# Layer 1's bias rows in three vector operations on all partitions, and new orders of work on three engines, in a fused GroupNorm, Hadamard and pointwise-MLP kernel

## The chip, the cores and the metric

One core of a Trainium2 chip runs the kernel. The metric is the time of one execution on the device in microseconds, lower is better. In the profile PE is TensorE's matmuls, PEld its weight loads, DVE VectorE, ACT ScalarE, POOL GpSimd and SP SyncE, which issues the DMAs.

## What is computed

The input x has 16 images of 192 channels and 56 x 56 points in fp32. The function is a pair of residual stages:

```
x  = x + hadamard(gn(x))           # per point: 192 channels times a Hadamard matrix
x1 = gn(x)                         # GroupNorm, 32 groups of 6 channels, no affine part
h  = gelu(layernorm(x1 @ W1.T + b1) * g1 + beta1)     # over the 192 channels of a point
h  = gelu(layernorm(h  @ W2.T + b2) * g2 + beta2)
out = x + (h @ W3.T + b3)
```

## The kernel before

**Tiling.** Two images make a pair (8 pairs). A pair's 192 channels lie as three blocks of columns: the first 128 channels of either image, and the last 64 of both, one image on the lower 64 partitions and one on the upper. A pair's 3136 points are cut into 7 units of 448, 56 units in all. Every fp32 operand of a matmul is split into an fp16 part and an fp16 remainder ("hi", "lo"); ACT makes the hi parts, DVE and POOL the lo parts.

**Stages of a unit.** Load; `stats_x` (DVE, GroupNorm 1's statistics, one instruction for each block); `scaled_hi` (ACT) and `scaled_lo` (DVE) make the scaled input `xs`; `h_ab` and `h_c` (PE) are the Hadamard matmuls; `residual` (DVE) adds them into X; `stats_x1` (DVE) is GroupNorm 2's statistics; `split_x1` (ACT) and `x1_split_lo` (DVE) make `x1`; then two layers, each in halves h = 0, 1 of 224 points: `group` (PE), `squares` (ACT), `rstd` (POOL), `normalise` (DVE), `transposes` (PE), `gelu` and `gelu_hi` (ACT), `gelu_lo` (POOL). `l3_ab` and `l3_c` (PE) are layer 3, `final_ab` and `final_c` (DVE) add them to X, and SP stores.

**The order.** Each engine runs a prologue (the first pair's GroupNorm 1, all its Hadamard units, the weights' preparation) and then `step(g)` for g = 0 to 57. A step's list of calls is written out by hand for each engine, and semaphores tie the lists together. Step g holds layer 1 of unit g, layer 2 of unit g - 1, layer 3 of unit g - 2 and the Hadamard stage of unit g + 8 (steps 6 to 47). Steps 2 and 4 hold a second Hadamard unit, named by `FIRST_H` in slot k = 1. The 21 statistics instructions 42 to 62 are dealt to steps 1 to 3 by `FIRST_STATS`.

**Shapes on PE.** The bias matmul (L402), L409, L320 and L356 work in tiles of 64 rows; L337 and L373 in tiles of 64 columns; L415, L315, L332, L351, L368 and the fp32 transposes (L427, L433) use the full height and width (112 rows for the transposes). PSUM has two banks `tm` for the layers, two `tp` for the transposes, and two `hl`, called "a" and "b", that the Hadamard stage, layer 3 and GroupNorm's small products share; `free` waits until the last reader of a bank is done.

**GroupNorm at a pair's border.** Once in seven steps each norm has its own work. GroupNorm 1 of pair q (steps 4, 11, 18, 25, 32, 39): `gn_stats` (DVE), `gn_means` (PE), `gn_var` (DVE), `groupnorm_rstd` (POOL), `gn_shift` (DVE), and in the next step `h_shift` (PE) and `gn_h_bias` (DVE). GroupNorm 2 (steps 6, 13, 20, 27, 34, 41, 48): the same chain, then `w1_shift` (PE) multiplies the shift by W1, and `gn_w1_bias` (DVE) makes layer 1's two bias rows (hi and lo) from it, on partitions 0, 1, 64 and 65. The next pair's first `group` (L402) waits for `s_bias` and for `s_x1_lo`. `ones` is one on those four partitions only, and zero elsewhere. The parameter column `row1` is 1 on partitions 1 and 65, so a row comes out as value minus hi on odd and as value on even ones, with the sign turned once more at the end.

Of the kernel before, what the change touches and what calls it, by code (L numbers as in the profile page):

```python
# [83 lines left out]
def build(nc, x, weights, biases, params, consts, out):  # L84
    ctx = ExitStack()
    with ctx:
# [575 lines left out]
        def _(dve):  # L662
# [141 lines left out]
            def gn_shift(q, n):  # L804

                if q is None:
                    return
# [3 lines left out]
                mu = gmu[:, 0, :]
                if n == 1:
                    do(nc.vector.tensor_tensor(gmu_b3[:, :], mu, b3, ALU.add))
                    mu = gmu_b3[:, :]
# [228 lines left out]
```

## Time and profile before

| what | value |
|---|---|
| time, median of 3 runs | 1047.11 us (1045.45 to 1048.05) |
| the profiled execution | 1043.52 us |
| its span, first to last instruction | 1041.7 us |
| PE busy | 932.8 us, 90% |
| ACT busy | 890.1 us, 85% |
| DVE busy | 868.4 us, 83% |
| POOL busy | 612.5 us, 59% |
| mean granted TensorE clock | 0.977 of full |
| DMA | 80.66 MB, mean 77 GB/s |

The span is what the trace covers, and the profiled execution took 1.8 us more than it. An engine's busy time is a mean over a prologue, 58 steps of several kinds and a tail, so the rows of single steps say more than the table.

### The profile page before, as it was taken

How to read it: one execution, taken by the hardware profiler on the slowest of the kernel's cores; microseconds unless marked ns; L12 is line 12 of the kernel's file. 1: busy time of each engine (PE TensorE's matmuls, PEld its weight loads, DVE VectorE, ACT ScalarE, POOL GpSimd, SP SyncE). 2: the span in 40 equal slices, each digit the busy share in tenths (PEclk: the TensorE clock that was granted, in tenths of full speed). 3: DMA queues.
4: the chain of work that ended last, by engine and by line, in shares of the span. 5: the costliest groups of instructions: out<-in, count | busy, mean ns of one | idle time of the engine just before them, and what ended most of it. 6: DMA issues, size and time to landing. Idle time of an engine off the chain costs nothing.

```text
span 1041.7 us, 25024 instructions
## 1 busy us (share of the span) xinstructions
PE 932.8 (90%) x9384; PEld 638.9 (61%) x9384; DVE 868.4 (83%) x1553; ACT 890.1 (85%) x2821; POOL 612.5 (59%) x477
## 2 busy tenths in 40 slices
PE   0637898999998999999998999999999999999995
PEld 0216565666666666666765666666676666677662
DVE  6798999998999899999899989999889877854542
ACT  0727887899988998899988998889998999899992
POOL 0533654566665667556665667566665666666662
PEclk9967999999999999999999999999999999999997
DMA  9524021132222222222322232222101111011111
GB/s 288 158 78 109 28 81 55 54 107 77 85 81 81 81 81 86 77 85 78 107 71 74 85 94 81 81 81 81 54 31 52 34 50 54 28 54 55 54 46 62
DMA packets 49080, 80.66 MB, mean 77 GB/s; under 512 B 5568, under 2 KB 48704, under 8 KB 48832
## 3 DMA queue, kind: packets, MB, share of 16 engines
q1 hardware_dynamic: 48960, 79.06, 24.8%
q8 instruction: 75, 1.23, 0.5%
q14 instruction: 45, 0.37, 0.1%
HBM read 40.51 MB, written 38.54 MB: 76 GB/s over the span
## 4 chain that ended last, share of the span: by engine, by line
PE 68%; DVE 22%; POOL 3%; ACT 2%; issue 2%; SPq 1%; DMA 1%; POOLq 0%; ACTq 0%; DVEq 0%
PE tm L415 18%; PE tp L427 9%; PE tm L409 8%; PE tm L402 5%; PE hl L351 5%; PE hl L315 4%; DVE z L871 3%; PE hl L373 3%; PE tp L433 3%; PE hl L356 3%; PE hl L368 3%; DVE X L745 3%; DVE bn L720 3%; DVE x_lo L861 2%; PE hl L320 2%; DVE xs_lo L736 2%
## 5 line engine op out<-in xcount | busy, mean ns | idle before, releaser
L626 POOL TENSOR_TENSOR ge_lo<-ge,ge_hi 128x672 f16<-128x672 f32 x224 | 334.5, 1494 | 131.4 <-ACT ge_hi L532 131.4
L617 POOL TENSOR_TENSOR rs<-ssq,neg_half 112x4 f32<-112x4 f32 x224 | 246.6, 1101 | 228.0 <-ACT z L503 228.0
L503 ACT ACTIVATE z<-tm 112x194 f32<-112x194 f32 x896 | 284.3, 340 | 29.0 <-PE tm L415 29.0
L871 DVE TENSOR_TENSOR z<-tm,rs 112x768 f32<-112x768 f32 x224 | 212.6, 949 | 55.7 <-POOL rs L617 54.2
L516 ACT ACTIVATE ge<-tp,par 128x448 f32<-128x448 f32 x224 | 163.6, 731 | 53.6 <-PE tp L427 45.6
L503 ACT ACTIVATION_READ_ACCUMULATOR z<-tm 112x1 f32 x896 | 194.9, 217 | 0.0
L532 ACT ACTIVATE ge_hi<-ge 128x672 f16<-128x672 f32 x224 | 174.4, 778 | 2.2
L427 PE MATMUL tp<-cst,z 112*128 112x112 f32 x896 | 134.9, 273 | 14.8 <-DVE z L871 13.0
L745 DVE SCALAR_TENSOR_TENSOR X<-hl,h_bias,X 128x448 f32<-128x448 f32 x161 | 105.0, 678 | 50.4 <-PE hl L320 42.3
L427 PEld LDWEIGHTS tp<-cst,z 112*128 112x128 f32 x896 | 89.5, 142 | 87.8 <-issue 59.6
L494 ACT ACTIVATE x_hi<-X,gscale 128x448 f16<-128x448 f32 x168 | 106.8, 671 | 21.2 <-DVE gscale L819 21.2
L519 ACT ACTIVATE ge<-tp,par 128x224 f32<-128x224 f32 x224 | 121.0, 540 | 0.0
L415 PE MATMUL tm<-w_hi,x_hi 128*112 128x192 f16 x448 | 116.2, 259 | 0.0
L415 PE MATMUL tm<-w_hi,ge_hi 128*112 128x192 f16 x448 | 115.1, 257 | 0.0
L736 DVE SCALAR_TENSOR_TENSOR xs_lo<-X,gscale,xs_hi 128x448 f16<-128x448 f32 x150 | 114.4, 769 | 0.8 <-ACT xs_hi L483 0.7
L415 PE MATMUL tm<-w_lo,x_hi 128*112 128x192 f16 x448 | 111.2, 248 | 0.0
L415 PE MATMUL tm<-w_hi,x_lo 128*112 128x192 f16 x448 | 111.1, 248 | 0.0
L861 DVE SCALAR_TENSOR_TENSOR x_lo<-X,gscale,x_hi 128x448 f16<-128x448 f32 x168 | 109.9, 683 | 1.2 <-ACT x_hi L494 0.9
L415 PE MATMUL tm<-w_lo,ge_hi 128*112 128x192 f16 x448 | 110.2, 246 | 0.0
L415 PE MATMUL tm<-w_hi,ge_lo 128*112 128x192 f16 x448 | 110.2, 246 | 0.0
L483 ACT ACTIVATE xs_hi<-X,gscale 128x448 f16<-128x448 f32 x150 | 99.9, 676 | 5.5 <-DVE gscale L819 5.5
L720 DVE BATCH_NORM_STATS2 bn<-X 128x6 f32<-128x448 f32 x168 | 100.0, 617 | 5.3 <-DMA X<-x 5.1
(138 smaller groups left out, 2181.5 us busy)
## 6 DMA issues: line engine op xcount, KB each, us to landing
X<-x SPq DMA_DIRECT2D x56, 448.0 KB, 3.7
out<-X SPq DMA_DIRECT2D x56, 448.0 KB, 2.7
X<-x SPq DMA_DIRECT2D x112, 112.0 KB, 3.7
out<-X SPq DMA_DIRECT2D x112, 112.0 KB, 2.8
X<-weights SPq DMA_DIRECT2D x1, 1024.0 KB, 12.2
cst<-consts SPq DMA_DIRECT2D x1, 704.0 KB, 9.7
X<-biases SPq DMA_DIRECT2D x1, 192.0 KB, 2.5
par<-params SPq DMA_DIRECT2D x1, 6.5 KB, 1.6
```

Of the source, the lines that this page charges most:

```text
L415: last = nc.tensor.matmul(dst[:, i, k * TW:k * TW + C], act[:, buf, i, cols], w[:, 3 * i, :], start=False, stop=(r == 2), skip_group_check ...
L427: last = nc.tensor.transpose(tp[:, 0, i * HALF + k * TT:i * HALF + (k + 1) * TT], z[n][:, 2 * h + k, at:at + 128], ident[0:TT, 0:TT])
L503: last = nc.scalar.activation(z[n][:, 2 * h + k, i * TW:(i + 1) * TW], tm[h][:, i, k * TW:(k + 1) * TW], ACT.Square, scale=float(C) ** -0. ...
L516: nc.scalar.activation(ge[n][:, 0:2, cols], tp[:, 0, 0:2 * HALF].rearrange("p (b t) -> p b t", b=2), ACT.Gelu, bias=par[:, 4 * n + 2:4 * n ...
L532: nc.scalar.activation(ge_hi[n][:, g % 2, :, cols], ge[n][:, :, cols], ACT.Copy).then_inc(s_ge_hi[n], 1)
L617: nc.gpsimd.tensor_tensor(rs[n][:, 2 * h:2 * h + 2, :], ssq[n][:, 2 * h:2 * h + 2, :], neg_half[0:TT, 0:4].rearrange("p (i k) -> p i k", i=2),
L626: nc.gpsimd.tensor_tensor(ge_lo[n][:, g % 2, :, cols], ge[n][:, :, cols], ge_hi[n][:, g % 2, :, cols], ALU.subtract).then_inc(s_ge_lo[n], 1)
L720: ins = nc.vector.bn_stats(bn[0][:, (a // U) % 2, b, a % U, :], xcols(a, b))
L736: ins = nc.vector.scalar_tensor_tensor(out=xs_lo[:, a % 2, b, :], in0=xcols(a, b), scalar=scale1(a // U, b), in1=xs_hi[:, a % 2, b, :], op ...
L745: nc.vector.scalar_tensor_tensor(out=xcols(a, b), in0=tp[:, 0, 0:UT] if b == 2 and a < U else hl[:, b % 2, 0:UT], scalar=h_bias[:, (a // U ...
L861: ins = nc.vector.scalar_tensor_tensor(out=x1_lo[:, g % 2, b, :], in0=xcols(g, b), scalar=gscale2[:, b:b + 1], in1=x1_hi[:, g % 2, b, :], ...
L871: nc.vector.tensor_tensor(z[n][:, 2 * h:2 * h + 2, 0:2 * C].rearrange("p k (i o) -> p i k o", i=2), tm[h][:, :, 0:2 * TW].rearrange("p i ( ...
```

## The change

Five edits. (1) `gn_w1_bias` works on all 128 partitions in three operations: subtract, cast to fp16, and one `scalar_tensor_tensor` that writes both copies of the rows; the parameter column is -1 where it was 1. `layer_biases` in the prologue is shortened the same way. (2) The shift has the other sign, so `gn_shift` needs no multiplication by -1; for GroupNorm 2 it adds `b3` in the same instruction, three instead of one and six. (3) The prologue has 7 instead of 10 statistics instructions ahead of step 0 and 14 instead of 11 in it, fewer of them ahead of `gn_var`, and makes the bias rows before the first `x1_split_lo`. (4) POOL's first `groupnorm_rstd(0, 1)` comes after the last weight remainder, no longer before it. (5) The step lists of PE, ACT, POOL and DVE are reordered.

```diff
-FIRST_STATS = {0: (42, 42), 1: (42, 52), 2: (52, 56), 3: (56, 63)}
+FIRST_STATS = {0: (42, 42), 1: (42, 54), 2: (54, 54), 3: (54, 63)}
 # PE step
     group(g, 0, 0)
+    transposes(g - 2, 1, 1)
     h_ab(h_unit(g, 0))
-    transposes(g - 2, 1, 1)
     group(g, 0, 1)
...
     transposes(g, 0, 1)
+    group(g - 1, 1, 1)
     w1_shift(gn2_pair(g))
-    group(g - 1, 1, 1)
     h_shift(h_shift_pair(g))
     l3_c(g - 2)
+    transposes(g - 1, 1, 0)
     h_ab(h_unit(g, 1))
-    transposes(g - 1, 1, 0)
     h_c(h_unit(g, 1))
 # ACT step: scaled_hi of slot 0 moves: block 0 between the first two squares,
 # block 2 behind gelu(g, 0, 0), ahead of split_x1(g + 1, 0); slot 1 is spread out
 # POOL step
     gelu_lo(g - 2, 1, 1)
+    rstd(g, 0, 1)
     groupnorm_rstd(gn2_pair(g), 1)
-    rstd(g, 0, 1)
 # DVE step, after the change
+    gn_stats(gn2_pair(g), 1)
+    first_stats(g)
+    gn_stats(gn1_pair(g), 0)
+    scaled_lo(xs_unit(g, 0), 0)
+    residual(h_unit(g, 0), 0)
+    residual(h_unit(g, 0), 1)
+    normalise(g, 0, 0)
+    stats_x1(h_unit(g, 0), 0)
+    stats_part(g, 0)
+    gn_var(gn2_pair(g), 1)
+    residual(h_unit(g, 0), 2)
+    gn_var(gn1_pair(g), 0)
+    scaled_lo(xs_unit(g, 0), 1)
+    gn_shift(gn2_pair(g), 1)
+    normalise(g, 0, 1)
+    scaled_lo(xs_unit(g, 0), 2)
+    x1_split_lo(g + 1, 0)
+    x1_split_lo(g + 1, 1)
+    final_ab(g - 2)
+    stats_x1(h_unit(g, 0), 1)
+    normalise(g - 1, 1, 0)
+    gn_shift(gn1_pair(g), 0)
+    scaled_lo(xs_unit(g, 1), 0)
+    gn_w1_bias(gn2_pair(g))
+    x1_split_lo(g + 1, 2)
+    gn_h_bias(h_shift_pair(g))
+    stats_part(g, 1)
+    final_c(g - 2)
+    normalise(g - 1, 1, 1)
+    stats_x1(h_unit(g, 0), 2)
+    residual(h_unit(g, 1), 0)
+    stats_part(g, 2)
+    scaled_lo(xs_unit(g, 1), 1)
+    residual(h_unit(g, 1), 1)
+    residual(h_unit(g, 1), 2)
+    stats_x1(h_unit(g, 1), 0)
+    scaled_lo(xs_unit(g, 1), 2)
+    stats_x1(h_unit(g, 1), 1)
+    stats_x1(h_unit(g, 1), 2)
 # gn_w1_bias, after the change
+    nc.vector.tensor_tensor(b_row[:, :], b32[:, :], gp[:, 0:C], ALU.subtract).then_inc(s_gread, 1)
+    dve.wait_ge(s_gread, reads)
+    do(nc.vector.tensor_copy(b_hi[:, :], b_row[:, :]))
+    nc.vector.scalar_tensor_tensor(out=bias_rows[0][:, :, 0:C],
+                                   in0=b_hi[:, :].unsqueeze(1).to_broadcast([128, 2, C]), scalar=low_row,
+                                   in1=b_row[:, :].unsqueeze(1).to_broadcast([128, 2, C]),
+                                   op0=ALU.mult, op1=ALU.add).then_inc(s_bias, 1)
 # DVE prologue
-            stats_x(range(21, 27))
+            stats_x(range(21, 24))
             gn_var(0, 1)
-            stats_x(range(27, 28))
+            stats_x(range(24, 26))
             gn_shift(0, 1)
-            stats_x(range(28, 31))
+            stats_x(range(26, 28))
+            gn_w1_bias(0)
             for b in range(3):
                 x1_split_lo(0, b)
-            gn_w1_bias(0)
```

## Rows read from the trace of the kernel before

**Rows 1.** Busy us by stretch: length, PE, PEld, DVE, ACT, POOL; then clock, DMA.
```profile
92.62:189.56 96.94, 85.25 (x833) 57.51 (x832) 89.06 (x150) 79.75 (x254) 50.36 (x40) 0.97 0.14 44
225.94:241.72 15.78, 15.78 (x166) 10.84 (x165) 13.99 (x22) 15.48 (x51) 10.28 (x9) 1.00 0.28 89
510.07:528.14 18.07, 16.87 (x172) 11.70 (x171) 16.70 (x34) 15.57 (x51) 13.11 (x11) 1.00 0.25 77
544.76:564.13 19.37, 17.64 (x181) 12.05 (x180) 18.20 (x52) 16.11 (x51) 10.37 (x10) 1.00 0.24 73
564.13:581.13 17.00, 15.95 (x164) 10.83 (x164) 16.58 (x24) 15.27 (x51) 9.89 (x8) 1.00 0.27 82
926.44:940.94 14.50, 13.58 (x150) 10.09 (x149) 7.32 (x10) 13.91 (x48) 9.73 (x9) 1.00 0.15 49
```
**Rows 2.** Timeline of PE, step 29: start us, us, engine, line, operation, tiles.
```profile
582.88 0.25 PE L415 MATMUL tm<-w_hi,x_lo 128*112 128x192 f16 x1
582.96 0.35 PE L315 MATMUL hl<-xs_hi,h 128*128 128x448 f16 x1
...
584.01 0.35 PE L320 MATMUL hl<-xs_lo,h 64*128 64x448 f16 x2
...
584.73 0.35 PE L433 MATMUL tp<-cst,z 112*128 112x112 f32 x2
585.02 0.37 PE L402 MATMUL tm<-bias,ones 64*112 64x388 f16 x2
```
**Rows 3.** Timeline of PE, steps 1 and 48, other neighbours of the same blocks.
```profile
96.87 0.35 PE L320 MATMUL hl<-xs_lo,h 64*128 64x448 f16 x2
97.06 0.33 PE L402 MATMUL tm<-bias,ones 64*112 64x388 f16 x2
...
896.79 0.55 PE L427 MATMUL tp<-cst,z 112*128 112x112 f32 x4
897.18 0.35 PE L433 MATMUL tp<-cst,z 112*128 112x112 f32 x2
```
**Rows 4.** Timelines of PE, DVE and POOL at pair 4's border, steps 27 and 28.
```profile
559.15 0.83 PE L296 MATMUL hl<-w,gshift 128*2 128x192 f32 x8 [1.49 <-DVE X L883]
...
560.32 0.70 DVE L841 TENSOR_TENSOR b_row<-hl,b 2x192 f32<-2x192 f32 x2
563.39 0.68 DVE L861 SCALAR_TENSOR_TENSOR x_lo<-X,gscale,x_hi 128x448 f16<-128x448 f32 x1
563.99 1.89 DVE L736 SCALAR_TENSOR_TENSOR xs_lo<-X,gscale,xs_hi 128x448 f16<-128x448 f32 x1
567.52 0.94 DVE L871 TENSOR_TENSOR z<-tm,rs 112x768 f32<-112x768 f32 x1
...
563.86 1.53 POOL L626 TENSOR_TENSOR ge_lo<-ge,ge_hi 128x672 f16<-128x672 f32 x1
```
**Rows 5.** Timelines of DVE and PE in step 25, GroupNorm 1 of pair 5.
```profile
522.37 2.42 DVE L817 SCALAR_TENSOR_TENSOR gshift<-gmu,gscale 128x2 f32<-128x2 f32 x3
...
526.03 0.36 PE L368 MATMUL hl<-ge_hi,w_hi 128*128 128x448 f16 x1 [1.20 <-DVE X L883]
```
**Rows 6.** Timeline of DVE, operations of the new rows' kinds, in the prologue.
```profile
5.16 0.26 DVE L691 CAST bias<-X 128x192 f16<-128x192 f32 x1
5.46 0.42 DVE L692 SCALAR_TENSOR_TENSOR X<-bias,par,X 128x192 f32<-128x192 f16 x1
```
**Rows 7.** Timeline of DVE, from the first pair's GroupNorm 2 into step 0.
```profile
66.56 0.15 DVE L797 COPY gmu<-hl 128x8 f32<-128x8 f32 x1
...
68.44 1.10 DVE L813 TENSOR_TENSOR gmu_b<-gmu,par 128x4 f32<-128x4 f32 x1 [0.60 <-POOL gscale L609]
...
76.68 5.89 DVE L720 BATCH_NORM_STATS2 bn<-X 128x6 f32<-128x448 f32 x11
```
**Rows 8.** Timelines of DVE and PE at the end of step 2, slot k = 1.
```profile
126.78 3.45 DVE L736 SCALAR_TENSOR_TENSOR xs_lo<-X,gscale,xs_hi 128x448 f16<-128x448 f32 x3
...
130.89 0.36 PE L332 MATMUL hl<-xs_hi,h 128*128 128x448 f16 x1 [1.80 <-DVE X L745]
```

More of the change, by code:

```diff
@@ L729, in first_stats @@
                 if g == 0:
-                    stats_x(range(31, 42))
+                    stats_x(range(28, 42))
             def scaled_lo(a, b):
@@ L807, in gn_shift @@
                     return
-                do = chain(q, n, 2)
                 dve.wait_ge(s_grs, gn_use(q, n) + 1)
                 scale = (gscale1[:, q % 2, :], gscale2[:, :])[n]
[L811 to L814, printed above, removed]
-                for rows, cols in ((slice(0, 128), slice(0, 2)), (lower[0], slice(2, 3)), (lower[1], slice(3, 4))):
-                    for i in range(n + 1):
-                        nc.vector.scalar_tensor_tensor(out=gshift[n][rows, cols, i], in0=mu[rows, cols], scalar=-1.0,
-                                                       in1=scale[rows, cols], op0=ALU.mult, op1=ALU.mult)
+                for rows, cols, w in ((slice(0, 128), slice(0, 2), 2), (lower[0], slice(2, 3), 1), (lower[1], slice(3, 4), 1)):
+                    if n == 0:
+                        nc.vector.tensor_tensor(gshift[0][rows, cols, 0], gmu[rows, 0, cols], scale[rows, cols], ALU.mult)
+                    else:
+                        shape = [rows.stop - rows.start, w, 2]
+                        nc.vector.scalar_tensor_tensor(out=gshift[1][rows, cols, :],
+                                                       in0=gmu[rows, 0, cols].unsqueeze(2).to_broadcast(shape),
+                                                       scalar=b3[rows, cols.start:cols.start + 1],
+                                                       in1=scale[rows, cols].unsqueeze(2).to_broadcast(shape),
+                                                       op0=ALU.add, op1=ALU.mult)
                 nc.vector.tensor_copy(scale[lower[1], 2:3], scale[lower[1], 3:4]).then_inc(s_gn[n], 1)
@@ L837, in gn_w1_bias @@
                 dve.wait_ge(s_gred, reads)
-                do = chain(q, 1, 3)
-                two = (slice(0, 2), slice(64, 66))
-                for rows in two:
-                    last = nc.vector.tensor_tensor(b_row[rows, :], gp[rows, 0:C], b32[rows, :], ALU.add)
-                last.then_inc(s_gread, 1)
-                dve.wait_ge(s_gread, reads)
-                for rows in two:
-                    last = nc.vector.tensor_copy(bias_rows[0][rows, 0, 0:C], b_row[rows, :])
-                do(last)
-                for rows in two:
-                    last = nc.vector.scalar_tensor_tensor(out=b_row[rows, :], in0=bias_rows[0][rows, 0, 0:C],
-                                                          scalar=row1[rows, :], in1=b_row[rows, :],
-                                                          op0=ALU.mult, op1=ALU.subtract)
-                do(last)
-                for rows in two:
-                    for k in range(2):
-                        last = nc.vector.tensor_scalar(bias_rows[0][rows, k, 0:C], b_row[rows, :], -1.0, None, ALU.mult)
-                last.then_inc(s_bias, 1)
+                do = chain(q, 1, 2)
+                nc.vector.tensor_tensor(b_row[:, :], b32[:, :], gp[:, 0:C], ALU.subtract).then_inc(s_gread, 1)
+                dve.wait_ge(s_gread, reads)
+                do(nc.vector.tensor_copy(b_hi[:, :], b_row[:, :]))
+                nc.vector.scalar_tensor_tensor(out=bias_rows[0][:, :, 0:C],
+                                               in0=b_hi[:, :].unsqueeze(1).to_broadcast([128, 2, C]), scalar=low_row,
+                                               in1=b_row[:, :].unsqueeze(1).to_broadcast([128, 2, C]),
+                                               op0=ALU.mult, op1=ALU.add).then_inc(s_bias, 1)
             def x1_split_lo(g, b):
@@ L906, in step @@
                 gn_shift(gn2_pair(g), 1)
-                stats_part(g, 0)
                 normalise(g, 0, 1)
+                scaled_lo(xs_unit(g, 0), 2)
                 x1_split_lo(g + 1, 0)
                 x1_split_lo(g + 1, 1)
-                gn_shift(gn1_pair(g), 0)
                 final_ab(g - 2)
```

52 lines of the change are left out of this document (20 added, 32 removed).

## The prediction

> **What bounds the kernel now.** I read the timeline of PE first and took the start of each unit's first bias matmul (L402) as the start of its step. That splits the span into a prologue of 76.8 us, steps 0 to 55 (938.5 us, nine tenths) and a tail. Then I read busy time by step. The stretches of [rows 1] are steps 1 to 5 together, then steps 8, 25, 27, 28 and 50. In a plain step, such as step 8, PE is busy for all of the 15.78 us, ACT for 15.48 and DVE for 13.99 [rows 1]. So PE sets the pace of a plain step, and only fewer or closer matmuls shorten it; ACT stands right behind. Of the 42 steps 6 to 47, those with Hadamard work, 20 are of this kind and length. The steps at a pair's border are longer, and there PE does wait: 19.37 us with 17.64 busy in step 27, 17.00 with 15.95 in step 28, and 18.07 with 16.87 in step 25 [rows 1]. Steps 1 to 5 take 96.94 us with PE busy for 85.25 and DVE for 89.06, so neither is full alone [rows 1]. From step 49 on there is no Hadamard work and a step takes 14.50 us with 13.58 of PE [rows 1]; there a chain of latencies rules, and its lists are the same before and after, since all calls that move are empty in those steps. I give these steps and the tail nothing.
>
> **Term 1, the order on PE in each Hadamard step.** The transposes of unit g - 2 move from behind h_ab to ahead of it. No matmul is removed, so only the gaps between neighbours can change. From the last L415 of the first group to L402 of the second it now takes 585.02 - 582.88 = 2.14 us [rows 2]. From the last L320 over four transposes to L433 it is 0.72, of which four transposes behind a group take 0.39; 0.33 are left, although the distance from L320 to L402, where those two are neighbours, is 0.19 [rows 2, 3]. L433 to L402 is 0.29 for two transposes, which by the 0.39 for four take about 0.2 [rows 2, 3]. In every case the longer gap stands where the matmul shape goes from 64-row tiles to the full array or back, and the full-to-full change L415 to L315 costs its plain 0.08 [rows 2]. In the new order the sum is 0.08 (group to transposes) + 0.39 + 0.22 to 0.29 (L433 to h_ab, no row shows it; 0.22 if it has no gap, like other full neighbours) + 1.05 (L315 to the last L320, unchanged) + 0.19 = 1.93 to 2.00. That is 0.14 to 0.21 us less; I take 0.18, as two of three gaps are read directly. For 42 steps: 7.6 us. The lower bound is 0, if the gap only moves. The page "TensorEngine Tiling (Array Packing)" of the Trainium skill, section Key Properties, says that changing the tiling mode drains the engine; by counting changes, 16 in a step become 14, it would give about the same.
>
> Do the others keep up at 15.60 us? ACT's 15.48 leaves 0.12. But it includes overlaps of neighbouring instructions, and its list is the same in sum. DVE first waits for h_ab, which now ends 0.7 us later in the step; it does one scaled_lo of 0.6 before it, so it loses nothing of its 1.8 us of slack. final_ab comes 0.6 us later, behind scaled_lo block 2; l3_c has 1.3 us between l3_ab's product being added and its own start, so it isn't delayed.
>
> **Term 2, the border of GroupNorm 2 (steps 6/7 to 41/42, six times).** Three waits. w1_shift waits 1.49 us for final_ab to free bank "b", with group(g-1, 1, 1) queued behind it [rows 4]. In the new list that group (1.83 us from its L402 on) goes first and covers the wait. gn_w1_bias took from 560.32 to 563.39 = 3.07 us of DVE [rows 4], with x1_split_lo block 2 behind it, for which the next group waits. New: the subtraction as one of L841's two, 0.35; the cast 0.26 [rows 4, 6]; the wide one has 384 elements, 0.42 for 192 [rows 6] to 0.84 for twice that, and I take 0.61, on the slope from 192 elements to the 448 of L861's 0.68 [rows 4]; with two waits of 0.04, 1.3 us. gn_shift saves some 0.4 more by four fewer small instructions. So DVE has 2.2 us less to do, and w1_shift starts 14.4 us into the step, as before. I walked the new lists with these durations: normalise(g, 0, 1) moves up by 1.1 us, since POOL's rstd now precedes the GroupNorm's; w1_shift ends 15.2 us after the step's start, bias rows are there at 16.6, x1_lo block 2 at 17.2, while PE itself is done at 17.25. The wait is gone to within 0.1. In step 28 PE waited 1.05 us, 17.00 less 15.95 [rows 1], at h_ab, because DVE was late: normalise at 567.52, behind a scaled_lo that took 1.89 instead of 0.68 [rows 4]. DVE's 2.2 us, and normalise(g-1, 1, 1) ahead of the statistics, put that at 1.9 us into the step, where PE asks for it at 1.8. A border then costs two plain steps plus PE's own small products: 36.37 becomes 33.5 before term 1, so 2.7 us saved, and 2.3 at 41/42, where no statistics run: 5 x 2.7 + 2.3 = 15.8. Bounds: 0 if each wait only moves, 3.1 a border if all goes.
>
> **Term 3, the border of GroupNorm 1 (steps 11, 18, 25, 32).** gn_shift took 2.42 us for three tiny instructions, and final_ab, queued behind it, held up l3_c by 1.20 us [rows 5]. Now final_ab, a statistic and a normalise stand ahead of it. What waits next is x1_split_lo block 2, 1.4 us before it is needed. 4 x 1.2 = 4.8 us; step 39 shows no such wait.
>
> **Term 4, step 48.** w1_shift waits as in step 27, 1.5 us [rows 4], and the step after it shows no wait that the change touches: 1.5.
>
> **Term 5, the prologue.** gn_var, now at 66.56, comes three statistics earlier; at 5.89 / 11 = 0.535 us each [rows 7] that is 1.6 us at most, of which I take 1.1, since GroupNorm's means on PE must be done first. gn_shift's first operation took 1.10 us for 0.16 of work, under POOL's last weight remainder [rows 7]; with edit (4) that is over before: 0.9. The merged shift gives 0.4 and the rows 1.8. Against it stand three statistics more in step 0, 1.6 us. 1.1 + 0.9 + 0.4 + 1.8 - 1.6 = 2.6 us. Edit (4) also lets SP, which waits for the last weight remainder, issue the third pair's loads some 9 us earlier; the statistics already find their data, so nothing more comes of it. layer_biases lies ahead of the first unit's landing: 0.
>
> **Term 6, steps 1 to 5.** In steps 2 and 4 three scaled_lo (3.45 us with a stall) stand between h_ab of the second unit and its residual, and h_c waits 1.80 us for it [rows 8]. Two of the three are now behind the residual. PE waited for 96.94 - 85.25 = 11.7 us in the five steps, DVE for 96.94 - 89.06 = 7.9 [rows 1]. The longer list is DVE's: 89.06, of which 2.8 are stalls of the two trios (3.45 each, where three at 0.68 take 2.04). Of its 7.9 us idle some half waits for step 1's first h_ab and stays. So 89.1 + 3.9 = 93.0 if the stalls stay, 90.2 if not; I take 92.5, a gain of 4.4 us, with bounds of 0 and 8.
>
> **The sum.** 7.6 + 15.8 + 4.8 + 1.5 + 2.6 + 4.4 = 36.7 us. The span of 1041.7 becomes 1005.0 and the profiled execution's 1043.52 becomes 1006.8. The median of the runs shown is 3.6 above that execution, so 1010.4; I say 1011.
>
> **Rivals.**
> *The waits move (A).* POOL's gelu_lo and DVE meet: the scaled_lo at 563.99 took 1.2 us more beside the gelu_lo from 563.86 [rows 4], while most others ran undisturbed. If the wide bias instruction, x1_split_lo behind it or the moved gn_shift meets it at each border, 1.2 us comes back at seven GroupNorm 2 borders (8.4), and steps 1 to 5 give nothing (4.4): 1011 + 12.8 = 1024. For it speaks that bias rows are now ready 1.9 us after w1_shift is issued, on the path; against it, that the walk puts POOL's gelu_lo elsewhere by 1 us. The Trainium skill, "GPSIMD Engine Reference", Key points, says GpSimd shares its SBUF interfaces with VectorE instructions that have two SBUF inputs, which the wide one has on 128 partitions. It speaks against edit (1), and the row above agrees.
> *The gaps stay (B).* If the gap of 0.1 belongs to the transposes and not to the change of shape, term 1 is 0: 1018.6. ACT as the new bound gives nearly the same: at 15.7 us a step, 0.1 of the 0.18 is lost in 42, and the time is 1015.
> *Slower (C).* The new PE list puts h_ab behind transposes that wait for normalise(g-2, 1, 1). So a loop closes in every step: that normalise, transposes 0.66, h_ab 1.24, then DVE from residual to the next such normalise, 13.99 less two statistics and one scaled_lo = 12.35, and latencies 0.3: 14.55 us. It is 1.05 under the 15.60 of PE. One stall of 1.2 us in the loop lengthens a step to 15.75 and eats term 1 alone; from two a step (16.95, 1.17 above before) the loss is 42 x 1.17 = 49 against the other terms' 29: 1067. It decides from 29 / 42 = 0.7 us above 15.78. Against it: in plain steps the trace shows scaled_lo at 0.68 to 0.78, one near-miss a step.
> *The change does nothing (D).* It would need A at full size and term 1 at 0 and 15 us more; I see no single mechanism.
>
> **How the numbers follow.** Forecast (all six terms near their size) 0.63, own range 1004 to 1018. A 0.17, B 0.11, D 0.03, C 0.06. The range that leaves out no more than 2 in 10 runs from 1001 (term 6 at its bound of 8, borders at 3.1, term 1 at 0.21: 5 to 8 us more) to 1026 (A). What a measurement of this kernel can tell from no change is about 0.3%, 3 us. Faster by more 0.91, within 0.03, slower 0.06.
>
> **What the profile after would show.** Step 8's kind at 15.57 to 15.64 us with PE full (term 1); L433 to L315 at 0.22. L296 without a wait, and borders of GroupNorm 2 at some 33.0 us for two steps. Step 25's kind at 16.7. First L402 near 72.5 and step 1 near 90.0. Wrong would be: plain steps above 15.8 with PE waiting at L427 for z (C); L402 of steps 7, 14, ... waiting for bias or x_lo by over 0.5 us (A); plain steps still 15.78 (B).

## The result, and the profile after

The changed kernel takes 1005.14 us (median of 4 runs, 1004.59 to 1005.64) against 1047.58 us before (median of 4 runs, 1045.45 to 1048.12). The ratio is 0.9598, with a 95% interval of 0.9582 to 0.9615: 4.0% faster. The profiled execution took 1005.64 us with a span of 1003.7; before they were 1043.52 and 1041.7. The spans differ by 38.0 us. The line numbers of the loop moved by a few: L402 is L404, L415 L417, L427 L429, L433 L435, L315 L317, L320 L322, L296 L298, L272 L274; L736 stays, L861 is L854, L871 L864, L883 L876.

Busy time by stretch, in the columns of [rows 1]: steps 1 to 5, then steps 8, 25, 27, 28 and 50, each from its first L404 to the next step's.

```profile
91.68:187.33 95.65, 86.51 (x832) 60.17 (x832) 87.76 (x153) 79.27 (x254) 51.86 (x40) 0.94 0.15 45
220.22:235.71 15.49, 15.49 (x164) 10.90 (x163) 14.05 (x22) 15.34 (x51) 9.75 (x9) 1.00 0.30 90
490.89:507.28 16.39, 16.39 (x173) 11.80 (x172) 15.88 (x36) 15.45 (x51) 11.16 (x10) 1.00 0.28 85
523.61:540.86 17.25, 17.25 (x181) 12.07 (x180) 16.87 (x39) 15.56 (x51) 10.26 (x9) 1.00 0.27 81
540.86:556.50 15.64, 15.64 (x165) 10.93 (x165) 15.05 (x23) 15.45 (x51) 9.78 (x9) 1.00 0.29 89
888.45:902.94 14.49, 13.58 (x150) 10.08 (x149) 7.30 (x10) 13.89 (x48) 9.71 (x9) 1.00 0.15 49
```

In all four steps of the loop PE is now busy from end to end. The plain step fell from 15.78 to 15.49 us, step 25 from 18.07 to 16.39, step 27 from 19.37 to 17.25 and step 28 from 17.00 to 15.64; step 50 did not move. ACT, at 15.34 of 15.49, is right behind PE. Steps 1 to 5 gave only 1.29 us, and their granted clock is 0.94 where it was 0.97.

The timeline of PE in step 30, which answers to [rows 2]:

```profile
573.74 0.25 PE L417 MATMUL tm<-w_hi,x_lo 128*112 128x192 f16 x1
573.82 0.55 PE L429 MATMUL tp<-cst,z 112*128 112x112 f32 x4
574.21 0.35 PE L435 MATMUL tp<-cst,z 112*128 112x112 f32 x2
574.40 0.35 PE L317 MATMUL hl<-xs_hi,h 128*128 128x448 f16 x1
...
575.45 0.35 PE L322 MATMUL hl<-xs_lo,h 64*128 64x448 f16 x2
575.64 0.33 PE L404 MATMUL tm<-bias,ones 64*112 64x388 f16 x2
```

From the last L417 to L404 it is now 575.64 - 573.74 = 1.90 us, where [rows 2] had 2.14. The transposes hand over to h_ab in 0.19 and h_ab's 64-row tiles to the 64-row bias matmul in 0.19.

The border of pair 4, which answers to [rows 4], on DVE and, last, on PE:

```profile
538.90 0.35 DVE L842 TENSOR_TENSOR b_row<-b,hl 128x192 f32<-128x192 f32 x1
539.29 0.26 DVE L844 CAST b_hi<-b_row 128x192 f16<-128x192 f32 x1
539.58 0.62 DVE L845 SCALAR_TENSOR_TENSOR bias<-b_hi,par,b_row 128x384 f16<-128x384 f16 x1
540.12 0.68 DVE L854 SCALAR_TENSOR_TENSOR x_lo<-X,gscale,x_hi 128x448 f16<-128x448 f32 x1
...
540.86 0.37 PE L404 MATMUL tm<-bias,ones 64*112 64x388 f16 x2
```

The bias rows take 540.12 - 538.90 = 1.22 us, where they took 3.07 [rows 4], and no line of PE in steps 27 and 28 shows idle time ahead of it.

PE in the prologue and step 0, with its idle time and what ended it in brackets:

```profile
73.29 0.57 PE L404 MATMUL tm<-bias,ones 64*112 64x388 f16 x2 [3.25 <-DVE x_lo L854]
82.15 1.87 PE L274 MATMUL hl<-gst,cst 128*128 128x4 f32 x8 [2.53 <-DVE gst L789]
85.78 0.98 PE L429 MATMUL tp<-cst,z 112*128 112x112 f32 x4 [0.53 <-DVE z L864]
```

The first step starts 3.5 us sooner (73.29, was 76.80), but then PE waits 2.53 us for the statistics (1.11 before), and its next eight small matmuls take 1.87 us, where the same eight took 1.05 before: the granted clock over them is 0.50, the lower of its two levels, and was 1.00. Step 1 starts at 91.68, only 0.94 sooner than the 92.62 of [rows 1].

### The profile page after: what moved, and what is told of

It is laid out like the page before. It is cut to its first block, busy times and chain, and to the rows that moved or that the text cites. A ratio compares the mean times of both kernels' runs of the same rounds, so it can differ in the third digit from the quotient of the medians.

```text
span 1003.7 us, 24928 instructions
## 1 busy us (share of the span) xinstructions
PE 921.3 (92%) x9384; PEld 645.5 (64%) x9384; DVE 839.9 (84%) x1462; ACT 883.2 (88%) x2821; POOL 595.9 (59%) x477
## 4 chain that ended last, share of the span: by engine, by line
PE 80%; DVE 9%; ACT 4%; POOL 3%; issue 1%; SPq 1%; DMA 1%; POOLq 0%; ACTq 0%
PE tm L417 22%; PE tp L429 10%; PE tm L411 10%; PE hl L353 6%; PE tm L404 5%; PE hl L317 4%; PE hl L375 4%; PE hl L358 4%; PE tp L435 4%; PE hl L370 3%; PE hl L322 2%; PE hl L339 2%; PE hl L334 2%; DVE bn L720 2%; PE hl L274 2%; POOL ge_lo L628 2%
## 5 line engine op out<-in xcount | busy, mean ns | idle before, releaser
L619 POOL TENSOR_TENSOR rs<-ssq,neg_half 112x4 f32<-112x4 f32 x224 | 234.5, 1047 | 251.7 <-ACT z L505 251.5
L628 POOL TENSOR_TENSOR ge_lo<-ge,ge_hi 128x672 f16<-128x672 f32 x224 | 328.6, 1467 | 90.6 <-ACT ge_hi L534 90.5
L864 DVE TENSOR_TENSOR z<-tm,rs 112x768 f32<-112x768 f32 x224 | 212.6, 949 | 57.7 <-POOL rs L619 56.2
L505 ACT ACTIVATION_READ_ACCUMULATOR z<-tm 112x1 f32 x896 | 203.8, 227 | 0.0
L534 ACT ACTIVATE ge_hi<-ge 128x672 f16<-128x672 f32 x224 | 176.7, 789 | 2.2
L429 PE MATMUL tp<-cst,z 112*128 112x112 f32 x896 | 133.3, 271 | 13.5 <-DVE z L864 12.3
L429 PEld LDWEIGHTS tp<-cst,z 112*128 112x128 f32 x896 | 91.1, 143 | 69.4 <-issue 39.4
L736 DVE SCALAR_TENSOR_TENSOR xs_lo<-X,gscale,xs_hi 128x448 f16<-128x448 f32 x150 | 107.0, 716 | 27.1 <-ACT xs_hi L485 27.0
L521 ACT ACTIVATE ge<-tp,par 128x224 f32<-128x224 f32 x224 | 123.1, 550 | 0.0
L417 PE MATMUL tm<-w_hi,x_hi 128*112 128x192 f16 x448 | 116.7, 261 | 0.0
L417 PE MATMUL tm<-w_hi,ge_hi 128*112 128x192 f16 x448 | 115.6, 258 | 0.0
L417 PE MATMUL tm<-w_lo,x_hi 128*112 128x192 f16 x448 | 111.7, 249 | 0.0
L417 PE MATMUL tm<-w_hi,x_lo 128*112 128x192 f16 x448 | 111.7, 249 | 0.0
L854 DVE SCALAR_TENSOR_TENSOR x_lo<-X,gscale,x_hi 128x448 f16<-128x448 f32 x168 | 109.9, 682 | 1.8 <-ACT x_hi L496 1.6
L417 PE MATMUL tm<-w_hi,ge_lo 128*112 128x192 f16 x448 | 110.7, 247 | 0.0
L417 PE MATMUL tm<-w_lo,ge_hi 128*112 128x192 f16 x448 | 110.7, 247 | 0.0
```

The source lines that it names most:

```text
L417: last = nc.tensor.matmul(dst[:, i, k * TW:k * TW + C], act[:, buf, i, cols], w[:, 3 * i, :], start=False, stop=(r == 2), skip_group_check ...
L429: last = nc.tensor.transpose(tp[:, 0, i * HALF + k * TT:i * HALF + (k + 1) * TT], z[n][:, 2 * h + k, at:at + 128], ident[0:TT, 0:TT])
L505: last = nc.scalar.activation(z[n][:, 2 * h + k, i * TW:(i + 1) * TW], tm[h][:, i, k * TW:(k + 1) * TW], ACT.Square, scale=float(C) ** -0. ...
L521: nc.scalar.activation(ge[n][:, 2, cols], tp[:, 1, 0:HALF], ACT.Gelu, bias=par[:, 4 * n + 3:4 * n + 4], scale=par[:, 4 * n + 1:4 * n + 2]) ...
L534: nc.scalar.activation(ge_hi[n][:, g % 2, :, cols], ge[n][:, :, cols], ACT.Copy).then_inc(s_ge_hi[n], 1)
L619: nc.gpsimd.tensor_tensor(rs[n][:, 2 * h:2 * h + 2, :], ssq[n][:, 2 * h:2 * h + 2, :], neg_half[0:TT, 0:4].rearrange("p (i k) -> p i k", i=2),
```

## The experiments

The diffs say from which of the two kernels each one starts. The lists that differ between the two are those of four engines, POOL's by one pair of lines. The table gives the lengths of five kinds of step in the profiled execution, in us, the start of step 6, and the median.

| kernel | 8 | 25 | 27 | 28 | 48 | step 6 starts | median |
|---|---|---|---|---|---|---|---|
| before | 15.78 | 18.07 | 19.37 | 17.00 | 17.19 | 189.56 | 1047.6 |
| after | 15.49 | 16.39 | 17.25 | 15.64 | 15.67 | 187.33 | 1005.1 |
| e1, h_ab first again | 15.78 | 16.67 | 17.54 | 15.78 | 15.64 | 191.59 | 1018.9 |
| e2, before + swap | 15.73 | 19.93 | 19.20 | 19.41 | 17.17 | 195.91 | 1082.3 |
| e3, narrow bias rows | 15.50 | 16.38 | 21.69 | 16.86 | 20.23 | 188.52 | 1053.2 |
| e4, w1_shift early | 15.49 | 16.39 | 18.67 | 15.50 | 17.12 | 187.25 | 1014.3 |
| e5, gn_shift 1 early | 15.50 | 16.38 | 17.24 | 15.65 | 15.67 | 185.06 | 1004.4 |
| e6, 64-row tiles first | 15.74 | 16.63 | 17.49 | 15.89 | 15.67 | 186.99 | 1014.0 |
| e7, old prologue | 15.50 | 16.39 | 17.25 | 15.64 | 15.67 | 183.58 | 1004.5 |
| e8, transposes before l3 | 15.79 | 16.73 | 19.49 | 15.61 | 20.18 | 188.29 | 1035.9 |
| e9, new forms, old lists | 15.78 | 18.06 | 18.83 | 15.78 | 16.97 | 189.05 | 1031.7 |
| e10, e5 and e7 together | 15.50 | 16.39 | 17.25 | 15.64 | 15.66 | 189.96 | 1006.9 |
| e11, e2 + early normalise | 15.74 | 21.18 | 19.09 | 18.88 | 17.18 | 202.47 | 1081.1 |
| e12, changed kernel again | 15.50 | 16.39 | 17.25 | 15.64 | 15.66 | 187.09 | 1004.0 |

### What does the swap on PE give? (e1, e6)

e1 puts h_ab ahead of the transposes again in the changed kernel; e6 keeps the swap and runs h_ab's 64-row tiles before its full ones, so that its neighbours on both sides change shape again.

```diff
 # e1, PE step
     group(g, 0, 0)
-    transposes(g - 2, 1, 1)
     h_ab(h_unit(g, 0))
+    transposes(g - 2, 1, 1)
 # e6, h_ab: the loop over 64-row tiles (start=True) moves ahead of the full ones
```

> The changed kernel with one line of TensorE's step put back: h_ab ahead of the transposes of unit g - 2. Theory (each change of matmul shape costs TensorE a gap of 0.1 us or so, and the new list has two fewer): a plain step goes from 15.50 back to 15.78 us, the whole from 1005 to about 1017. Rival (the plain step became shorter because VectorE's and ScalarE's lists are better): a plain step stays at 15.5 to 15.6, the whole at 1005 to 1009.

> The changed kernel with the inner order of h_ab turned: its matmuls in 64-row tiles first, the full ones last. Same matmuls and neighbours as blocks, two changes of shape more in each Hadamard step. Theory (the gap goes with the change of shape): a plain step of 15.50 becomes 15.70 to 15.78, the whole 1014 to 1017. Rival (the gap belongs to the fp32 transposes or to what stands beside them): no change in the step, 1005.

e1: 1018.9 us, ratio 0.9744 (0.9724 to 0.9764), the plain step back at 15.78. e6: 1014.0 us, 0.9703 (0.9676 to 0.9731), plain step 15.74. PE has no wait in the plain step of either. One order of calls with two more changes of shape costs 0.24 us a step, the whole swap 0.28. In step 30 of e6 both new gaps can be seen:

```profile
579.69 0.35 PE L435 MATMUL tp<-cst,z 112*128 112x112 f32 x2
579.98 0.36 PE L318 MATMUL hl<-xs_hi,h 64*128 64x448 f16 x2
...
581.04 0.35 PE L322 MATMUL hl<-xs_lo,h 128*128 128x448 f16 x1
581.32 0.37 PE L404 MATMUL tm<-bias,ones 64*112 64x388 f16 x2
```

Both handovers took 0.19 in the changed kernel; they are 0.29 and 0.28 here. The transposes stand at the same place in both kernels, so the gap belongs to the change of shape and not to the transposes. That is the rule that the prediction named from the Trainium skill, "TensorEngine Tiling (Array Packing)", section Key Properties (changing the mode drains the engine); the runs agree with it.

### Is the loop of rival C real? (e2, e11)

e2 makes only the swap in the kernel before. e11 moves one line of DVE's list in it as well, the late normalise.

```diff
 # e2 and e11, PE step of before
     group(g, 0, 0)
+    transposes(g - 2, 1, 1)
     h_ab(h_unit(g, 0))
-    transposes(g - 2, 1, 1)
 # e11 alone, DVE step of before
     final_c(g - 2)
+    normalise(g - 1, 1, 1)
...
-    normalise(g - 1, 1, 1)
     stats_part(g, 2)
```

> The kernel before with only that one pair of TensorE's step swapped: the transposes of unit g - 2 ahead of h_ab. If TensorE's gaps are all that counts, a plain step goes from 15.78 to 15.50 and the whole from 1047.6 to about 1036. If VectorE's old list matters, the loop h_ab, residual, everything up to normalise(g - 1, 1, 1), transposes, h_ab closes at some 13.46 + 0.66 + 1.24 + 0.3 = 15.67 us, and the whole is about 1043.

> The kernel before with the swap on TensorE, and one line of VectorE's list moved: normalise(g - 1, 1, 1) stands directly behind final_c(g - 2) and not near the end of the list. The swap alone made the kernel 36 us slower, with TensorE waiting 2.4 us and 1.2 us for z in the step behind a border. Theory: that is the loop of transposes, h_ab, residual and the late normalise; with the normalise early the transposes find z ready, the plain step is 15.50 us, the steps of the borders come back to about those of before less the gap (17.0 and 17.8 us), and the kernel takes 1031 to 1038 us. Rival: the 36 us come from something else that the swap moves (the release of tp, ScalarE's order, the stall beside GpSimd's ge_lo): over 1050 us, with the steps behind the borders still 19 to 21 us.

e2: 1082.3 us, ratio 1.035 (1.0327 to 1.0373), far beyond both numbers expected. The same swap that is worth 13.8 us in the new lists (1018.9 less 1005.1) costs some 36 in the old ones (1082.3 less 1046.1, the median of before beside it). e2 in step 28, PE first and then DVE:

```profile
592.32 0.60 PE L427 MATMUL tp<-cst,z 112*128 112x112 f32 x4 [2.39 <-DVE z L871]
598.26 0.60 PE L427 MATMUL tp<-cst,z 112*128 112x112 f32 x4 [1.24 <-DVE z L871]
...
587.80 1.89 DVE L736 SCALAR_TENSOR_TENSOR xs_lo<-X,gscale,xs_hi 128x448 f16<-128x448 f32 x1
591.33 0.94 DVE L871 TENSOR_TENSOR z<-tm,rs 112x768 f32<-112x768 f32 x1
594.40 1.28 DVE L745 SCALAR_TENSOR_TENSOR X<-hl,h_bias,X 128x448 f32<-128x448 f32 x2 [1.60 <-PE hl L320]
595.59 1.74 DVE L736 SCALAR_TENSOR_TENSOR xs_lo<-X,gscale,xs_hi 128x448 f16<-128x448 f32 x1
597.26 0.94 DVE L871 TENSOR_TENSOR z<-tm,rs 112x768 f32<-112x768 f32 x1
```

PE asks for z one h_ab earlier, and DVE, late from the border, has it at 592.27. Then DVE itself waits 1.60 us for the later h_ab, because the old list puts the residuals at its top, and the stalled scaled_lo and normalise(g, 0, 0) behind them make PE wait 1.24 more. In step 25 the same order delays gn_stats, which stands behind the residuals, and PE waits 1.25 us for it at L272. Both engines wait for each other in turn.

e11: 1081.1 us, ratio 1.0336 (1.0314 to 1.0357). The theory, that the late normalise closes the loop, failed, and the rival's numbers held. Its step 28 and, last, the plain step 30:

```profile
590.46 1.88 DVE L736 SCALAR_TENSOR_TENSOR xs_lo<-X,gscale,xs_hi 128x448 f16<-128x448 f32 x1
593.46 0.95 DVE L871 TENSOR_TENSOR z<-tm,rs 112x768 f32<-112x768 f32 x1
594.46 0.60 PE L427 MATMUL tp<-cst,z 112*128 112x112 f32 x4 [1.86 <-DVE z L871]
600.40 0.60 PE L427 MATMUL tp<-cst,z 112*128 112x112 f32 x4 [1.24 <-DVE z L871]
...
629.08 1.27 DVE L745 SCALAR_TENSOR_TENSOR X<-hl,h_bias,X 128x448 f32<-128x448 f32 x2 [1.59 <-PE hl L320]
631.87 0.60 PE L427 MATMUL tp<-cst,z 112*128 112x112 f32 x4 [0.17 <-DVE z L871]
```

Its place took 0.53 us off the first wait (2.39 to 1.86), one statistics instruction, and nothing off the second. Even the plain step waits 0.17 us for z(g, 0, 0), and takes 15.74. The other two links stay: residuals and scaled_lo between h_ab and normalise(g, 0, 0), and the border's long DVE work. The new lists have the first scaled_lo and gn_stats ahead of the residuals. That these two moves are what makes the swap pay is not shown.

A part of the 36 us is the clock. e2's steps 21 and 28, in the columns of [rows 1], have the same work:

```profile
463.93:485.03 21.10, 18.70 (x163) 12.86 (x163) 16.48 (x24) 15.48 (x51) 9.38 (x8) 0.84 0.22 67
587.94:607.35 19.41, 15.78 (x163) 10.93 (x164) 17.44 (x24) 15.45 (x51) 9.45 (x8) 1.00 0.23 72
```

Each has a wait of 2.4 us at its first transposes; in step 21 the granted clock fell behind it (0.50 from 468 to 474 us) and the step took 1.7 us more, in step 28 it stayed at 1.00.

### What do the wide bias rows give? (e3, e9)

e3 brings the ten narrow operations back into the changed kernel, on partitions 0, 1, 64 and 65. e9 is the opposite: the new forms (edits 1, 2, 4 and the prologue of edit 3) with every step list and `FIRST_STATS` of before.

```diff
 # e3, gn_w1_bias of the changed kernel: for rows in (slice(0, 2), slice(64, 66))
-    nc.vector.tensor_tensor(b_row[:, :], b32[:, :], gp[:, 0:C], ALU.subtract)     # and the two behind it
+    ...     # 2 tensor_tensor, 2 tensor_copy, 2 scalar_tensor_tensor, 4 tensor_scalar
-LINKS = ((2, 2, 0), (3, 2, 1))
+LINKS = ((2, 2, 0), (3, 2, 2))
```

> The changed kernel with gn_w1_bias on partitions 0, 1, 64 and 65 again, in the ten instructions of before (3.07 us against 1.2). Theory (w1_shift ends 15.2 us into the border step and the bias rows and x1_split_lo block 2 behind it are just in time): the next group waits 1.8 us more at each of seven borders, some 12 us in all, 1017. Rival (VectorE has slack there): under 3 us, 1005 to 1008.

> The kernel before with the new forms alone (bias rows in three wide operations, the shift with the other sign, the new prologue of VectorE), every step list of the four engines and the counts of statistics as they were. Theory, by the terms of the prediction without the swap on TensorE: each of the seven GroupNorm 2 borders gives back the 1.8 us between ten narrow operations (3.07 us) and three wide ones (1.30 us), and the 1.2 us stall of the scaled_lo behind them goes or stays with where ge_lo falls, so 13 to 20 us in all; the plain step stays at 15.78 us: 1027 to 1034 us. Rival 1, the forms carry everything but the swap: the whole of the border terms and of the prologue, 26 us and more, 1018 to 1021 us. Rival 2, the new forms only pay with the new lists, since the border waits for something else in the old ones (X of final_ab, 1.49 us): under 7 us, 1039 to 1047 us.

e3: 1053.2 us, ratio 1.0082 (1.006 to 1.0104), slower than before and 48 us above the changed kernel, some 7 us for each of seven borders, where the operations alone differ by 1.8. Its border on DVE, POOL and PE, and the two microseconds behind it in the columns of [rows 1]:

```profile
562.75 2.25 DVE L851 SCALAR_TENSOR_TENSOR b_row<-bias,par,b_row 2x192 f32<-2x192 f16 x2
565.03 2.06 DVE L857 TENSOR_SCALAR bias<-b_row 2x192 f16<-2x192 f32 x4
...
563.34 1.46 POOL L628 TENSOR_TENSOR ge_lo<-ge,ge_hi 128x672 f16<-128x672 f32 x1
565.36 1.46 POOL L628 TENSOR_TENSOR ge_lo<-ge,ge_hi 128x672 f16<-128x672 f32 x1 [0.56 <-ACT ge_hi L534]
...
567.86 0.57 PE L404 MATMUL tm<-bias,ones 64*112 64x388 f16 x2 [4.38 <-DVE x_lo L864]
...
568.00:570.00 2.00, 2.00 (x18) 1.66 (x19) 1.99 (x4) 0.00 (x0) 0.00 (x0) 0.50 0.04 13
```

The rows took 567.12 - 561.46 = 5.66 us and not 3.07. L851's pair and L857's four took 0.83 and 0.89 in the kernel before; here each pair or four met one ge_lo of POOL (over at 564.80 and 566.82) and ended 0.2 to 0.3 us after it, at 565.00 and 567.09. x_lo and PE stand behind them, PE idles 4.38 us, and the clock falls to half. So 1.8 us of work and 2.6 of stall made the border step 4.4 us longer, 21.69 for 17.25. The slow clock made the step behind it 1.2 us longer here and 2.1 to 2.8 at the five other borders of this kind (it took 17.69 to 18.41 us there, with PE busy throughout and a clock of 0.83 to 0.87). The three wide operations are over before the next ge_lo begins, at 541.04 in the changed kernel.

e9: 1031.7 us, ratio 0.9863 (0.9843 to 0.9884), in the range expected (1027 to 1034). Its two border steps:

```profile
538.94:557.77 18.83, 17.50 (x182) 12.04 (x181) 17.81 (x44) 15.79 (x51) 10.06 (x9) 1.00 0.25 74
557.77:573.55 15.78, 15.78 (x165) 10.83 (x165) 13.82 (x22) 15.49 (x51) 10.15 (x9) 1.00 0.28 88
```

They became 34.61 us from 36.37, 1.76 less: 0.54 in step 27, where the wait for x_lo at the end is gone (0.25 us at L402 of step 28 in the kernel before) and the wait at w1_shift is 1.33 us for 1.49, and 1.22 in step 28, where PE's 1.05 us at h_ab is gone with the stall (DVE's scaled_lo took 0.68, no longer 1.89). That the total is near the 1.85 us between the two forms of the rows is thus no proof that it is this difference: most of it is a wait that the stall of scaled_lo had made. The wait at w1_shift and that at layer 3 in step 25 (1.19 us) are still there.

### The moves at the borders (e4, e5)

```diff
 # e4, PE step of the changed kernel
+    w1_shift(gn2_pair(g))
     group(g - 1, 1, 1)
-    w1_shift(gn2_pair(g))
 # e5, DVE step of the changed kernel
+    gn_shift(gn1_pair(g), 0)
     final_ab(g - 2)
...
-    gn_shift(gn1_pair(g), 0)
```

> The changed kernel with w1_shift ahead of group(g - 1, 1, 1), as before. Theory (w1_shift then waits for final_ab to free its bank, with that group behind it): a wait of 1.0 to 1.5 us at seven borders, 7 to 10 us in all, 1012 to 1015. Rival (the earlier bias rows pay for it): 1005 or less.

> The changed kernel with gn_shift of GroupNorm 1 ahead of final_ab again. Theory (its tiny instructions stall beside gelu_lo and hold up final_ab and l3_c): 1.2 us at four or five borders, 5 to 6 us in all, 1010 to 1011. Rival (in the new order GpSimd's work lies elsewhere, so there is no stall): 0 to 1 us, 1005 to 1006.

e4: 1014.3 us, ratio 0.9702 (0.9682 to 0.9722). L298 waits for final_ab's X again, 1.46 us, and the two border steps take 34.17 us, not 32.89. So of the gain at a border, 1.28 is this move and 1.76 the new forms of e9.

e5: 1004.4 us, 0.9607 (0.9586 to 0.9628), and the step of GroupNorm 1 unchanged. In it gn_shift is short although it stands where it stood before:

```profile
500.57 0.39 DVE L813 TENSOR_TENSOR gshift<-gmu,gscale 128x2 f32<-128x2 f32 x3
...
500.72 1.01 POOL L619 TENSOR_TENSOR rs<-ssq,neg_half 112x4 f32<-112x4 f32 x1 [1.85 <-ACT z L505]
501.70 1.47 POOL L628 TENSOR_TENSOR ge_lo<-ge,ge_hi 128x672 f16<-128x672 f32 x1
```

It is over 0.7 us before ge_lo starts, where in [rows 5] it had 2.42 us. The gain of GroupNorm 1's step came with the new lists (e9 does not have it), and in them it does not hang on the place of gn_shift. Whether the move of gn_shift alone would bring it in the old lists is not shown.

### A further order on PE (e8)

```diff
 # e8, PE step of the changed kernel
     group(g - 1, 1, 0)
+    transposes(g, 0, 1)
     l3_ab(g - 2)
-    transposes(g, 0, 1)
     group(g - 1, 1, 1)
```

> The changed kernel with transposes(g, 0, 1) ahead of l3_ab, which takes two more changes of shape out of every step, 0.28 us. But normalise(g, 0, 1) ends about 0.4 us after TensorE would ask for it. If that wait stands in full, a plain step is 15.6 to 15.7 and the whole 1010 to 1014; if the lists shift against each other and ScalarE's 15.2 us of work is the floor, 15.2 to 15.3 and 993 to 997.

1035.9 us, ratio 0.9907 (0.9887 to 0.9926). Neither expectation held. The shapes do fit together, but the transposes lose l3_ab as their cover. The plain step of e8, DVE's normalise(g, 0, 1) and the transposes:

```profile
595.18 0.96 DVE L864 TENSOR_TENSOR z<-tm,rs 112x768 f32<-112x768 f32 x1 [0.24 <-POOL rs L619]
596.19 0.60 PE L429 MATMUL tp<-cst,z 112*128 112x112 f32 x4 [0.36 <-DVE z L864]
```

The transposes start 0.60 us behind the last L417 of the group, 0.52 more than the 0.08 of [rows 2], against the 0.24 that two changes of shape less give back: 15.79 for 15.50. From step 43 to 46 the same wait is 0.74 us and a step takes 16.17; at a border it is 1.12, with 1.12 more for x_lo.

### The prologue (e7, e10, e12)

e7 gives the changed kernel VectorE's old prologue and its counts (10 statistics ahead of step 0, 11 in it); the new forms stay. e10 has the edits of e5 and e7. e12 is the changed kernel once more.

```diff
 # e7 and e10
-                    stats_x(range(28, 42))
+                    stats_x(range(31, 42))
...
-            stats_x(range(21, 24))
+            stats_x(range(21, 27))
             gn_var(0, 1)
-            stats_x(range(24, 26))
+            stats_x(range(27, 28))
             gn_shift(0, 1)
-            stats_x(range(26, 28))
-            gn_w1_bias(0)
+            stats_x(range(28, 31))
             for b in range(3):
                 x1_split_lo(0, b)
+            gn_w1_bias(0)
```

> The changed kernel with the old order in VectorE's prologue: ten statistics ahead of step 0 and eleven in it, bias rows behind x1_split_lo. Edit (4) and the short forms stay. Theory (the new prologue starts step 0 earlier, but VectorE has to do three statistics more in it, and TensorE idles and loses its clock): the first group starts 1.5 to 2 us later, step 1 within 0.5 us of the changed kernel's 91.7, the whole 1004.5 to 1006. Rival (the earlier start reaches the end): 1007.

> The changed kernel with both edits that each gave a microsecond or nothing at the median alone (VectorE's old prologue with its old counts of statistics; gn_shift of GroupNorm 1 ahead of final_ab). Theory: both spare TensorE a fall to the lower clock in steps 0 to 4, and in a place of its own each, so steps 0 and 4 take 15.6 and 23.2 us instead of 18.4 and 25.3, and the rest stays as it is: 3 to 5 us less than the changed kernel, 1000 to 1002 us. Rival: step 4 waits for VectorE whatever stands ahead of it and the old prologue already took that time (its step 4 was 23.7 us), so nothing is added to the old prologue's result: 1003 to 1005 us.

> The changed kernel itself, beside the one with the old prologue on the same chip, to compare these two directly. Nothing is changed. Theory: 1003 to 1006 us, steps 0 and 4 at 18.4 and 25.3 us in the profile if the fall of the clock in the prologue comes back in every execution. Rival: the fall was one execution's, and steps 0 to 5 are shorter by 2 us and more here.

e7: 1004.5 us (1000.6 to 1007.7), ratio 0.9608 (0.9578 to 0.9639). e10: 1006.9 us (1005.0 to 1008.4), 0.9627 (0.9606 to 0.9649). e12: 1004.0 us (1002.7 to 1005.5), 0.9601 (0.9582 to 0.9621). The intervals overlap, so none of the three can be told from another. In e7's profile PE waits less for the statistics, and the eight matmuls behind it still run at the higher clock, unlike the row at 82.15 above:

```profile
80.93 1.05 PE L274 MATMUL hl<-gst,cst 128*128 128x4 f32 x8 [0.54 <-DVE gst L789]
```

Its step 0 takes 15.55 us, not 18.39, and step 1 starts at 89.25. But e10, with the same prologue and a step 0 of 15.54, lost it again: its first step started at 76.37 (73.70 in e7; 1.6 us of the difference stood already behind the first pair's loads), step 1 took 18.03 (17.20 in e12) and step 4 took 26.28 with a clock of 0.79 over 150 to 160 us. The profiled execution of e7 is the fastest of its four and that of e10 the slowest, so their profiles lie further apart than their medians. In e12 steps 0 and 4 came back at 18.39 and 25.25. The changed kernel's fall of the clock in step 0 is thus no accident of one execution, but avoiding it gives nothing at the median.

## Why the prediction was right

The forecast was 1011 us with a range of 1001 to 1026, and 1005.1 was measured, inside the forecast's own range of 1004 to 1018. By its own sum, the profiled execution should have taken 1006.8 us and took 1005.6. So the terms together missed by 1.2 us, and that is in part luck: terms 1 to 3 gave 6.5 us more than foreseen and terms 4 to 6 gave 5.3 less. The forecast's further 3.6 us were added because the median of before lay that far above its profiled execution; after the change the profiled execution lay 0.5 above its median, so this step only took the forecast away from the result. Term by term, from the lengths of the steps in the two traces:

| term | predicted | measured | how measured |
|---|---|---|---|
| 1, order on PE | 7.6 | 11.8 | 0.28 x 42 |
| 2, border of GroupNorm 2 | 15.8 | 17.3 | 5 x (3.49 - 0.56) + 3.16 - 0.56 |
| 3, border of GroupNorm 1 | 4.8 | 5.6 | 4 x (1.68 - 0.28) |
| 4, step 48 | 1.5 | 1.0 | 1.52 less, 0.47 more in step 49 |
| 5, up to step 1 | 2.6 | 0.9 | 92.62 - 91.68 |
| 6, steps 1 to 5 | 4.4 | 1.3 | 96.94 - 95.65 |
| sum | 36.7 | 37.9 | spans: 38.0 |

**Term 1** was right in kind and too small: 0.28 us a step, above its bound of 0.21, and a plain step of 15.49 where 15.57 to 15.64 was expected. L435 to L317 was 0.19, below the 0.22 to 0.29 taken for it, because two transposes take 0.19 and not the 0.2 and more read from [rows 2]. The stretch gave 2.14 - 1.90 = 0.24. Most of the other 0.04 lies behind L404: from L404 to the first L417 it is 0.76 (575.64 to 576.40) where the bias matmul follows a matmul of its own shape, and 0.79 (579.13 to 579.92) where it follows transposes. e6 puts 0.24 of the 0.28 down to the shape. ACT did keep up, with 15.34 us busy. Rival B is refuted by e1 and e6.

**Term 2** is confirmed, also in its parts. The walk had the bias rows ready 16.6 us into the step and x1_lo block 2 at 17.2; in step 27 they were ready at 16.59 and 17.19 (540.20 and 540.80 less 523.61), and the next L404 started at 17.25. 1.76 us of a border come from the new forms (e9), most of it the wait at h_ab that hung on the stall of scaled_lo, and 1.28 from the group ahead of w1_shift (e4). Their sum, 3.04, is about the 2.93 measured beyond term 1.

**Term 3**: the size was near, the reason given for it not borne out. The stall of gn_shift is gone, but it stays gone with gn_shift in its old place (e5). In e5 ge_lo begins only 0.7 us after it, so where ge_lo falls decides, and the other moves had shifted that. Which of their lines did it stays open.

**Terms 5 and 6** failed, 4.8 us too much together. The first step did start 3.5 us sooner, where 4.2 was counted on; of the missing part some 0.5 us is the loads' time: the statistics of the last Hadamard unit ended that much later in the profiled execution of after. Against it the prediction set 1.6 us for three statistics more in step 0. PE's wait there did grow by 1.42, but the prediction left out that the clock can fall behind it, and 2.57 us are spent again in step 0 (18.39 for 15.82). In steps 1 to 5 step 2 gave 1.41 and step 5 1.19, and step 4 took 1.19 back. The wait that term 6 was about did shrink, from 1.80 to 0.86 us in step 2 and to 0.78 in step 4, but step 4 got another one, ahead of h_c of its first unit:

```profile
154.41 0.36 PE L334 MATMUL hl<-xs_hi,h 128*128 128x448 f16 x1 [1.90 <-DVE X L745]
```

The new list has gn_stats ahead of the residuals, and DVE, with its extra statistics, comes to them late; before, PE waited 0.80 us for gn_stats at this place. The waits of step 4 are 4.40 us in all, where they were 4.22, and the clock over 150 to 160 us is 0.85 where it was 1.00. e7 has the same 1.91 us wait with a clock of 1.00, and its step 4 takes 23.66 us, not 25.25: so some 1.6 us of that step is the clock, and it does not fall in every execution.

**Rival A** did not come about in the changed kernel, and e3 shows how near it was. The prediction feared the wide instruction beside GpSimd; it was the long row of narrow ones, in the new lists of e3, that met ge_lo, twice. The Trainium skill, "GPSIMD Engine Reference", Key points, says that GpSimd contends with VectorE instructions that have two SBUF inputs or run in a 2-port performance mode. The rows of e3 agree as to the first. L857, with one SBUF input, stalled as well; whether it ran in that mode no row shows.

**Rival C** was rightly set aside for this change, since PE is busy throughout in every stretch of the loop above. But the coupling that it names is real: in e2 PE's list and DVE's wait for each other in turn. It did not cost there what rival C priced: the plain step became no longer (15.73), the 36 us fell at the borders and in steps 1 to 5, and the late normalise, with which rival C closes its loop, was not what made them (e11). The prediction's point that DVE "loses nothing", as it does one scaled_lo ahead of the residual, holds for the new list only.

## What to carry to other kernels

Two edits of an order are not two terms of a sum: the swap on PE was worth 14 us in one set of lists and cost 36 in another. Before a producer is moved, look at what the consumer's list has directly ahead of its wait. When lists are packed to the end, count the changes of matmul shape, and shorten what DVE does at a place where the whole chain hangs on it; where a shorter operation just fits between two GpSimd instructions and the longer one does not, as in e3, the gain is more than the difference of their own times.

## What the runs showed of the hardware

- **A change of matmul shape costs about 0.1 us.** Full neighbours and 64-row neighbours of 448 columns follow at 0.19; from the last transposes to the 64-row bias matmul it is 0.28 to 0.29. A pair of changes a step is worth 0.24 (e6) to 0.28 us (e1).
- **VectorE stands still beside GpSimd's subtraction, by kind of input.** In the trace of after, from step 6 on, 36 scaled_lo (L736, both inputs in SBUF) began while a ge_lo ran, and each took 0.80 to 0.83 us and ended 0.48 us after it; otherwise they took 0.67 to 0.70. All 132 normalise (L864, one input in PSUM) and 193 statistics instructions that overlapped a ge_lo took their plain 0.94 to 0.96 and 0.60 to 0.62 us. In e3, four narrow L857 with a single SBUF input took 2.06 instead of 0.89. The order of the two matters: in the trace of before, from step 6 on, five scaled_lo were already running when a ge_lo began, and took their plain 0.68 us, and the ge_lo took 1.63 to 1.64 instead of 1.46.
- **Short waits can cost the clock, and do not always.** A wait of 2.53 us in step 0 of after was followed by small matmuls at the lower level (1.2 GHz, a granted clock of 0.50), and one of 1.90 us in step 4 by a clock of 0.85 over 150 to 160 us, in e7 by one of 1.00; in e2 the same wait of 2.4 us was followed by a clock of 0.84 over one step and of 1.00 over another.
